# A graph network's segment softmax on one Trainium2 core: state rows turned by TensorE instead of VectorE, and z split by node groups

## The reference

```python
msg = jax.nn.relu(h[src] + edge_attr) + EPS_MSG
m = msg * t
seg_max = jax.lax.stop_gradient(jax.ops.segment_max(m, dst, num_segments=N))
ex = jnp.exp(m - seg_max[dst])
denom = jax.ops.segment_sum(ex, dst, num_segments=N)
alpha = ex / (denom[dst] + 1e-16)
agg = jax.ops.segment_sum(msg * alpha, dst, num_segments=N)
out = h + agg
z = jax.nn.relu(_layernorm(out @ w1 + b1, g1, bb1))
return z @ w2 + b2
```

## Time and profile before

| | us |
|---|---|
| median of 3 runs | 4217.13 |
| lowest, highest | 4204.82, 4222.44 |
| the profiled execution, its own time | 4254.22 |
| its span | 4252.4 |
| mean granted TensorE clock | 0.778 of full speed |

### The profile page before, as it was taken

One profiled execution on the slowest core, in us unless ns is written; L12 is line 12 of the kernel. 1 busy time (PEld: TensorE's weight loads), 2 busy tenths in 40 slices (PEclk: granted clock), 3 DMA queues, 4 the chain that ended last, 5 costly groups with the idle time before them and its releaser, 6 DMA issues.

```text
span 4252.4 us, 48618 instructions
## 1 busy us (share of the span) xinstructions
PE 2955.6 (70%) x18494; PEld 1343.3 (32%) x18494; DVE 2769.2 (65%) x2608; ACT 1652.7 (39%) x2251; POOL 2537.0 (60%) x2651
## 2 busy tenths in 40 slices
PE   4766676776367777777657777777756777777774
PEld 2323232333223333333333333333323333333333
DVE  4766687777646666666765666666673666666668
ACT  1544453344423333333433333333343333333345
POOL 5665665655365565665565556666655655565655
PEclk7877787778577887887767877778867888877886
DMA  5787787887547777777656777777763777777764
GB/s 165 211 221 194 217 216 199 202 217 188 144 150 197 194 205 204 202 201 197 146 157 174 200 189 202 208 198 203 203 146 124 208 200 196 194 204 200 205 165 83
DMA packets 1041513, 800.46 MB, mean 188 GB/s; under 512 B 913146, under 2 KB 934655, under 8 KB 1015616
## 3 DMA queue, kind: packets, MB, share of 16 engines
q1 hardware_dynamic: 934480, 454.32, 46.3%
q10 hardware_dynamic: 23776, 246.29, 16.2%
q0 software_dynamic: 83024, 96.75, 9.3%
HBM read 498.09 MB, written 299.01 MB: 187 GB/s over the span
## 4 chain that ended last, share of the span: by engine, by line
PE 54%; issue 24%; DVE 12%; another core or an unknown queue 5%; ACT 4%; POOL 1%; SPq 1%; DMA 0%; DVEq 0%; POOLq 0%; ACTq 0%
PE X L643 44%; PE X L624 5%; PE X L653 3%; DVE decay L1008 3%; DVE state_all L1023 2%; DVE X L1013 1%; DVE rows_all L994 1%; DVE one_hot L1110 1%; ACT X L766 1%; DVE state_all L1039 1%; ACT msg L764 1%; DVE x_sb L1101 1%; POOL between L552 1%; PE X L677 0%
## 5 line engine op out<-in xcount | busy, mean ns | idle before, releaser
L525 POOL DMA_INDIRECT gath<-z_table,idx x2432 | 2352.0, 967 | 1526.1 <-issue 726.2
L643 PE MATMUL X<-one_hot,z_parts 128*64 128x512 fp8e5 x9450 | 1490.6, 434 | 669.2 <-issue 521.5
L643 PEld LDWEIGHTS X<-one_hot,z_parts 128*64 128x64 bf16 x9450 | 654.9, 122 | 1532.8 <-issue 1060.1
L643 PE MATMUL X<-between,z_parts 128*64 128x512 fp8e5 x5400 | 844.2, 425 | 309.5 <-issue 297.0
L1006 DVE TENSOR_TENSOR decay<-decay,top 128x1 f32<-128x1 f32 x216 | 34.2, 158 | 1329.3 <-ACT X L766 1255.8
L764 ACT ACTIVATE msg<-X,edge_bias 128x1024 f32<-128x1024 f32 (+2 forms) x216 | 228.5, 1058 | 1619.0 <-remote 1123.9
L643 PEld LDWEIGHTS X<-between,z_parts 128*64 128x64 bf16 x5400 | 371.9, 119 | 788.3 <-issue 606.7
L776 ACT ACTIVATE decay<-X 128x1024 f32<-128x1024 f32 (+2 forms) x216 | 209.3, 969 | 855.4 <-issue 515.1
L994 DVE STREAM_TRANSPOSE rows_all<-state_all 128x1024 f32<-128x1024 f32 (+3 forms) x432 | 505.7, 1171 | 9.6 <-DMA rows_table<-rows_all 2.1
L1008 DVE TENSOR_TENSOR_SCAN decay<-X,decay 128x1023 f32<-128x1023 f32 (+2 forms) x216 | 477.2, 2209 | 7.7
L1023 DVE TENSOR_TENSOR_SCAN state_all<-decay,state_all,X 128x1024 f32<-128x1024 f32 (+2 forms) x216 | 468.2, 2167 | 20.0 <-issue 10.7
(11 more groups left out here) (180 smaller groups left out, 1218.8 us busy)
## 6 DMA issues: line engine op xcount, KB each, us to landing
rows_table<-rows_all SPq DMA_DIRECT2D x784, 256.0 KB
attr<-attr_t SPq DMA_DIRECT2D x196, 512.0 KB
one_hot<-one_hot_dram ACTq DMA_DIRECT2D x39, 1920.0 KB
between<-one_hot_dram ACTq DMA_DIRECT2D x36, 1920.0 KB
one_hot<-one_hot_dram ACTq DMA_DIRECT2D x39, 1280.0 KB
one_hot_dram<-one_hot SPq DMA_DIRECT2D x25, 1920.0 KB
between<-one_hot_dram ACTq DMA_DIRECT2D x36, 1280.0 KB
gath<-z_table,idx POOLq DMA_INDIRECT x2432
```

What stands on the lines that cost most here:

```text
L525: pool.indirect_dma_start(out=gath[s][:, n * F:(n + 1) * F], out_offset=None, in_=z_table, in_offset=bass.IndirectOffsetOnAxis(ap=idx[:, c ...
L643: last = nc.tensor.matmul(x[h * F:(h + 1) * F, BANK:CH], z_parts[:, i * GB + k, third, :], bank[:, k, i, h * BANK:(h + 1) * BANK], start=F ...
```

## The change

It has three parts.

**Turning by TensorE.** The odd chunks 3 to 47 of layer 0 and chunks 49 to 53 of every layer (`turned_by_pe`) lose VectorE's two stream transposes. TensorE transposes the state in 128x128 tiles into the chunk's own X buffer (`turn_piece`, L716 of the new file), and ScalarE copies each half to `rows_all` (`copy_rows`, L871 and L875). In layer 0 this happens two chunks later: the denominators' eight transposes behind the rows of the odd chunk c + 2, then piece 2 of a chosen chunk's part 1 (30 matmuls), then, once ScalarE has copied the denominators (`den_copied`), the numerators' eight, then the other 60 matmuls. The edge product that stood there goes behind the next even chunk's rows and waits for ScalarE's second copy (`rows_ready`). On ScalarE both copies stand between an odd chunk's messages and its exponents. The numerators' copy ends the chunk's part on ScalarE and lets SyncE store. The stored pieces are 1 KB (`stored_rows`), where they were 256 bytes. The last five chunks have places of their own in `rows_all` (`row_place`), and their copies stand on ScalarE three chunks later, those of 51 to 53 after the ends' exponential. The padding behind the last column of the table is stored once, in layer 0, by a DMA of its own.

**z by groups.** In layers 1 to 3 the split is done for each of the seven node groups (`split_group`), 35 instructions on 256 or 192 columns instead of 5 on 1600, all after the last group's z.

**Chunk 0's product tile by tile.** `add_by_groups` issues its 150 matmuls in the order of the groups, 24 or 18 for each, behind that group's split. The edge product of chunk 1 now stands behind them.

```diff
+def turned_by_pe(layer, c):
+    return c > LAST_FULL or layer == 0 and c % 2 == 1 and 3 <= c
...
+def turned_up_to(layer, c):
+    return sum(turned_by_pe(k, m) for k in range(layer + 1) for m in range(NCH) if k < layer or m <= c)
...
+                sp.wait_ge(rows_ready[g % 2], g // 2 + 1)
+                if turned_by_pe(layer, c):
+                    k, k0 = n * SQ // P, row_place(c) // (HALVES * 2 * F)
+                    for a in parts:
+                        sp.dma_start(stored_rows(c, k, a), rows_by_tile[g % 2][a * SQ:(a + 1) * SQ, k0:k0 + k, :]).then_inc(stored[g % 2], 16)
+                    return
...
@@ -461,6 +490,9 @@
                     if layer == LAYERS - 1 and c == 0:
                         sp.wait_ge(built, NB1H * GB)
                         sp.dma_start(x_sb[:, :, :], x_nodes).then_inc(nodes_landed, 16)
+                    if layer == 0 and c == NCH - 1:
+                        past = rows_table[COLS * HALVES:BOUNDARY_ROW, :].rearrange("(k p h) e -> p k (h e)", p=P, h=HALVES)
...
+                if layer == 0 and part == 0 and c == chosen(layer)[0]:
+                    pe.wait_ge(z_split, 1)
...
-                for k in range(*PARTS[part]):
+                a, b = PARTS[part]
+                for k in range(max(a, b - only_last), b - but_last):
...
+            def add_by_groups(layer):
+                x = X[layer * NCH % XS]
+                for part in range(len(PARTS)):
+                    pe.wait_ge(hot_landed[hot_slot(0)][part], 16 * (loads_before(layer, 0) + 1))
+                for i, (t0, n) in enumerate(GROUPS):
+                    pe.wait_ge(z_split, 1 + split_before(layer, i))
+                    for t in range(t0, t0 + n):
+                        for third in range(3):
+                            for h in range(HALVES):
+                                last = nc.tensor.matmul(x[h * F:(h + 1) * F, BANK:CH], z_parts[:, t, third, :],
+                                                        hot[hot_slot(0)][:, t % GB, t // GB, h * BANK:(h + 1) * BANK], start=False,
+                                                        stop=(i == NG - 1 and t == t0 + n - 1 and third == 2))
+                last.then_inc(used, GB)
...
+            def turn_rows(layer, c):
+                g = layer * NCH + c
+                for q, ready in enumerate((den_ready, num_ready)):
+                    pe.wait_ge(ready, g + 1)
+                    turn_piece(layer, c, q, BANK if q == 0 else 0)
+
+            def turn_piece(layer, c, q, at):
+                g = layer * NCH + c
+                for k in range(tiles(c)):
+                    last = nc.tensor.transpose(X[g % XS][:, at + k * P:at + (k + 1) * P], state[g % 2][:, q, k * P:(k + 1) * P],
+                                               ident[:, :])
+                last.then_inc(pieces_turned, 1)
...
             for layer in range(LAYERS):
+                edge_product(layer, 0)
                 if layer > 0:
+                    add_by_groups(layer)
                     pe.wait_ge(h_added, layer * NG)
-                edge_product(layer, 0)
                 edge_product(layer, 1)
-                if 0 in chosen(layer):
-                    add_by_one_hot(layer, 0, 0)
-                    add_by_one_hot(layer, 0, 1)
                 for c in range(NCH):
                     add_rows(layer, c)
+                    if c == LAST_FULL + 3:
+                        turn_rows(layer, c - 2)
                     if layer > 0 and c + 1 in chosen(layer):
                         add_by_one_hot(layer, c + 1, 1)
-                    if c + 2 < NCH:
+                    if layer == 0 and c % 2 == 0 and turned_by_pe(layer, c - 3) and c <= LAST_FULL + 2:
+                        edge_product(layer, c + 1)
+                    if c + 2 < NCH - 1 and not (layer == 0 and turned_by_pe(layer, c - 2) and c <= LAST_FULL + 1):
                         edge_product(layer, c + 2)
-                    if layer == 0 and c + 1 in chosen(layer):
+                    if c == NCH - 2:
+                        edge_product(layer, NCH - 1)
+                    if layer == 0 and turned_by_pe(layer, c - 2) and c <= LAST_FULL + 1:
+                        pe.wait_ge(num_ready, c - 1)
+                        turn_piece(layer, c - 2, 0, 0)
+                        if c + 1 in chosen(layer):
+                            add_by_one_hot(layer, c + 1, 1, but_last=2)
+                        pe.wait_ge(den_copied, turned_up_to(layer, c - 2))
+                        turn_piece(layer, c - 2, 1, 0)
+                        if c + 1 in chosen(layer):
+                            add_by_one_hot(layer, c + 1, 1, only_last=2)
+                    elif layer == 0 and c + 1 in chosen(layer):
                         add_by_one_hot(layer, c + 1, 1)
                     if c + 2 in chosen(layer):
                         add_by_one_hot(layer, c + 2, 0)
...
                 w = width(NCH - 1)
+                turn_rows(layer, NCH - 4)
                 pe.wait_ge(last_max, g + 1)
-                pe.wait_ge(num_ready, g - XS + 2)
+                pe.wait_ge(rows_ready[(g - XS + 1) % 2], (g - XS + 1) // 2 + 1)
                 nc.tensor.matmul(ends_at(layer)[:, 0:P], top[g % 2][:, :], ident[:, :], start=True, stop=True).then_inc(ends_t, 1)
+                turn_rows(layer, NCH - 3)
+                turn_rows(layer, NCH - 2)
                 pe.wait_ge(num_ready, g + 1)
                 for n in range(2):
                     last = nc.tensor.matmul(ends_at(layer)[:, (n + 1) * P:(n + 2) * P], state[g % 2][:, n, w - 1:w], ident[:, :],
                                             start=True, stop=True)
                 last.then_inc(ends_t, 1)
+                turn_rows(layer, NCH - 1)
                 pe.wait_ge(ends_ready, layer + 1)
+                for k in (g - 1, g):
+                    pe.wait_ge(rows_ready[k % 2], k // 2 + 1)
...
+            def copy_rows(layer, c):
+                g = layer * NCH + c
+                w, late = width(c), turned_up_to(layer, c)
+                act.wait_ge(stored[g % 2], STORES_PER_LAYER[g % 2] * layer + 16 * NSTORE * (c // 2 - (c > LAST_FULL + 2) - (c == NCH - 1)))
+                at, den_at = row_place(c), BANK if w <= BANK else 0
+                to = rows_all[:, g % 2].rearrange("p b q j -> p (b q j)")[:, at:at + 2 * w].rearrange("p (m q j) -> p m q j", q=2, j=SQ)
+                act.wait_ge(pieces_turned, 2 * late - 1)
+                nc.scalar.activation(to[:, :, 0, :], X[g % XS][:, den_at:den_at + w].rearrange("p (m j) -> p m j", j=SQ), ACT.Copy)\
+                    .then_inc(den_copied, 1)
+                act.wait_ge(pieces_turned, 2 * late)
+                act.wait_ge(den_copied, late)
+                nc.scalar.activation(to[:, :, 1, :], X[g % XS][:, 0:w].rearrange("p (m j) -> p m j", j=SQ), ACT.Copy)\
+                    .then_inc(rows_ready[g % 2], 1)
...
                     messages(layer, c)
+                    if layer == 0 and turned_by_pe(layer, c - 2) and c <= LAST_FULL + 1:
+                        copy_rows(layer, c - 2)
+                    if LAST_FULL < c - 3:
+                        copy_rows(layer, c - 3)
...
                 nc.scalar.activation(ends_exp[:, :], ends_shift[:, :], ACT.Exp).then_inc(ends_exped, 1)
+                copy_rows(layer, NCH - 3)
+                copy_rows(layer, NCH - 2)
+                copy_rows(layer, NCH - 1)
...
-                    dve.wait_ge(stored[g % 2], STORES_PER_LAYER[g % 2] * layer + 16 * NSTORE * (c // 2))
-                turn_state(layer, c, 0, den_turned)
+                if not turned_by_pe(layer, c):
+                    if g >= 2:
+                        dve.wait_ge(stored[g % 2], STORES_PER_LAYER[g % 2] * layer + 16 * NSTORE * (c // 2))
+                    turn_state(layer, c, 0, den_turned)
                 dve.wait_ge(weighted, g + 1)
                 if g >= 1:
                     dve.wait_ge(num_ready, g)
                 v.tensor_tensor_scan(out=state[g % 2][:, 1, 0:w], data0=decay[s][:, 0:w], data1=X[g % XS][:, 0:w],
                                      initial=state[(g - 1) % 2][:, 1, before - 1:before], op0=ALU.mult, op1=ALU.add).then_inc(num_ready, 1)
-                dve.wait_ge(num_ready, g + 1)
-                dve.wait_ge(den_turned, g + 1)
-                turn_state(layer, c, 1, rows_ready)
+                if not turned_by_pe(layer, c):
+                    dve.wait_ge(num_ready, g + 1)
+                    dve.wait_ge(den_turned, g + 1 - turned_up_to(layer, c))
+                    turn_state(layer, c, 1, rows_ready[g % 2])
...
+            def split_group(layer, i):
+                t, n = GROUPS[i]
+                r, z3 = rest[i % 2][:, 0:n, :], z_parts[:, t:t + n, :, :]
+                if i < NG - 1:
+                    dve.wait_ge(z_ready, (layer - 1) * (NG - 1) + i + 1)
+                else:
+                    dve.wait_ge(z_last, layer)
+                d = Steps(split_steps, 4 + ((layer - 1) * NG + i) * 4)
```

(11 more changed lines are left out.)

53 lines of the change are left out of this document (29 added, 24 removed).

## The result

| | before | changed |
|---|---|---|
| median, us (4 runs each) | 4210.98 | 4336.26 |
| lowest, highest | 4203.14, 4222.44 | 4330.28, 4343.62 |
| profiled execution: span | 4252.4 | 4338.0 |
| layer 0, chunk 2 to chunk 48 | 941.26 | 1008.85 |

The ratio is 1.0279 (95% interval 1.0251 to 1.0307), against a forecast of 4227 us, a ratio of 1.002. The time lies above the range and beyond all but the worst form of rival (d), for which the prediction had 4330 us.

The account below looks back on a forecast made before the run. No engine is full, so the order of waits bounds the kernel, GpSimd's gathers setting the rhythm. Terms +25 - 15 + 0 = +10 gave 4264 us for the profiled execution, 4227 taken to the median; range 4130 to 4285.

Parts of the forecast that it names:

- rival (d): Layer 0: ScalarE's second copy, caught behind stalled TensorE, delays exponents; seven more long pairs 4282 us, all 4330; chance 0.24.
- Nine long pairs: Layer 0's pairs of chunks in the first profile: nine long (mean 46.2 us), thirteen short (mean 38.3), the last 27.6.
- Term 1: Layer 0's 23 pairs, odd chunks turned by TensorE: +25 us, present mix of long and short pairs kept.
- VectorE idles 8 to 10 us, so I price this at nothing.: Layer 0's odd chunks: copies delay the denominator scan 1 to 1.5 us; idle time absorbs it, otherwise 1 us a pair.
- The 46 records: Layer 0: eight transposes, 30 matmuls and eight more ahead of ScalarE's second copy, reached 3.8 to 21.8 us after L764.
- TensorE's +25 us: Layer 0, odd to even chunk: eight more records of 0.137 us, 1.1 us a pair over 23 pairs.
- Term 2: Last five chunks of each layer, where VectorE works back to back: -15 us; bounds nothing and -25.
- Term 3: Start of layers 1 to 3: the product starts 7.3 us earlier but still ends with the gather burst; 0 us.
- (a): Starts of layers 1 to 3: product gets through the burst, 25 us a layer gained, 4152 us; chance 0.13.
- (c): Layer 0 is bound by DMA, so 1 KB store pieces instead of 256 bytes give 4110 us; chance 0.06.
- Rival (b): Layer 0: TensorE's turn and lighter VectorE make all long pairs short, 4156 us; chance 0.17.

Follow-up runs that it names:

- TensorE's part alone: Kernel without odd chunks turned, plus 16 constant-tile transposes a layer-0 pair and moved edge products, no copies: 1.0108 with the stall; 1.0024 and 1.0020 without.
- without the waits: The change with layer 0's odd chunks turning and copying a constant tile, ScalarE and TensorE not waiting for each other: 1.0204; 1.0014 in a session without the stall.

## Why the prediction was wrong

*What bounds the kernel.* The reading of the pairs was right for that execution, but its layer 0 was 26 us above the mean of five. "Nine long pairs" were one to five in the others.

*Term 1, "I take the present mix, since the burst that makes it is not touched".* This is the step that failed. I count as long an odd chunk from 5 to 47 whose messages start more than 17 us before the next even chunk's. There were 9 of 22 in the first profile of before, 1 to 5 in the four others, 3 with TensorE's part alone, 12 without the waits, and 18 to 20 in the change. The burst was not touched, but everything around it had moved. Rival (d) (0.24) had the mechanism, if not all of it, and the measured time is near its case of all pairs (4330 us), not that of seven more. That the two numbers agree is in part luck: the 4330 took the tail for 15 us of gain, and the tail lost 12.

*"VectorE idles 8 to 10 us, so I price this at nothing."* The idle time was there. The delay was 8.5 us on average (exponents 15.0 us after the messages instead of 6.5; 22.8 in the stretch shown), not 2.2, and the copies without their waits gave 0.2. The smaller reading of this term held: the even chunks' scan waits for the exponents, 1.64 us a pair, so VectorE gains little from the transposes that it is spared.

*The 46 records.* I had counted where TensorE's records lie. ScalarE does not see a result when its record ends: in the stretch above it saw the first half 21 us later. A wait on TensorE in this kernel must be priced by when other engines see the result, and the lag was in my own rows: ScalarE saw chunk 41 at 922.94, its rows were recorded at 913.52 to 914.6.

*TensorE's +25 us.* No run speaks against it: 2 us by the profiles of other sessions (917 against 915), about 26 by the estimate from its own session. The 275 ns a transpose of the Trainium skill ("TensorE: Matmul & The Clock Gate", Part 4), in series, would have been further off, with its estimate of 51. In sessions without the stall even 32 transposes a pair cost nothing that can be told (ratio 1.0009).

*SyncE's queue.* The prediction did not follow it. The store of a turned chunk waits for ScalarE's copy, and `keep` and the edge attributes stand behind it. The penalties' wait for `keep` stands in 21 or 22 places in each kernel with the copies in layer 0 (70 to 84 us; 200 with the copies later) and nowhere in those without. It does not all lie on the path. In the change ScalarE goes on from the penalty to the next chunk's messages without idle time in all 22 cases, and by TensorE's records of the rows these messages could have started up to 63 us earlier in sum. Without the waits it is 7 cases and up to 17 us. In a session without the stall the same waits (92 us) cost nothing that can be told.

*Term 2, -15 us.* Wrong in sign: +12 between the first two profiles (with the split in it), +25 in the run without odd chunks. The way from chunk 48 on is meant, in all four layers. The subtraction was right as far as VectorE's own work goes. It left out the state's two slots: the scan of chunk c waits until chunk c - 2 is copied, and ScalarE copies chunk c - 2 only behind the messages of chunk c + 1. The scan of chunk 51 in layer 1:

```profile
2225.59 0.75 DVE L1124 TENSOR_TENSOR_SCAN state_all<-decay,state_all,X 128x256 f32<-128x256 f32 x1 [2.39 <-issue]
```

```profile
2224.86 0.60 ACT L875 ACTIVATE rows_all<-X 128x512 f32<-128x512 f32 x1
```

It waited 2.39 us, until the copy of chunk 49 ended at 2225.46. With that wait loosened, layers 1 to 3 came out even. In layer 0 GpSimd started 12.7 us after the boundary row and not 4.9: the large pieces did not help. The row's store went out at 1180.5, a microsecond behind the one-hot loads for layer 1, and from 1180 to 1190 the DMA engines were full (share 1.02 at 362 GB/s). That these loads held it up fits, and was not tested.

*Term 3, nothing:* right, by the mechanism given. *Rivals (a) and (c)* are out: the split alone gave 1.0006, and a DMA share of 0.68 instead of 0.78 made nothing faster. *Rival (b)* is out too: the long pairs became more.

*What stays open.* Of layer 0's 98 us, the waits between ScalarE and TensorE are 34 to 47 (the change against the kernel without them), and TensorE's added work 2 to 26. The remaining 25 to 60 are in the kernel without waits, which has late stores on SyncE's queue, copies on ScalarE, and no transposes on VectorE. Two readings were not parted. One is SyncE's queue, which explains by the count above at most 17 us there directly. The other is the rhythm of the bursts, which is argued from counts and not shown. Of the odd chunks 5 to 45 in the six profiles in which exponents come in time, all 12 that were seen less than 23 us after the even one had a long stretch behind them, and only 11 of the 114 others. In the kernel without waits 8 of 21 came under 23, all long, and 4 of the 13 others. VectorE, freed of transposes, starts the even chunk's maximum 2.4 us after its messages instead of 3.5, and so the odd chunk comes earlier, while the first burst still runs. A kernel with the copies at their place and the transposes kept would help to tell, in a session with the stall; the two runs of it met none. Nor was the change run in a session without the stall.

No version tried beats the kernel before. The nearest are the split alone (1.0006) and the tail with the loosened wait (1.0028), which are no difference.

## What to carry to other kernels

Before moving work from a busy engine to two idle ones, follow the new wait through every in-order queue it stands in: here ScalarE's, which held the exponents, and SyncE's, whose late store held the loads queued behind it. The added work itself was the smaller part (2 to 26 of some 100 us for TensorE's). Price a wait on TensorE by when its consumers start in the trace, not by its records. And take a second profile before counting a mix of long and short periods.

## What was unexpected of the hardware

TensorE's stall during bursts of indirect gathers is not a fixed property of kernel or chip. The same kernel took 4203 to 4349 us in four sessions and 3443 to 3462 in three, one chip having had both. In these three the stall was absent (0.0 us idle before layer 1's product) at nearly the same time a gather (967 to 971 ns against 958 to 968), with a mean granted clock of 0.82 to 0.83 against 0.77 to 0.79. What makes the difference was not found; DMA was at a 14% share in a stalled stretch, and a quarter of the gathers takes most of it away.
